# Gated stage: GpSimd's low parts interleaved and ternary weights in three steps; last stage: rows rounded at once, input rows turned ahead

## The chip, the cores and the metric

The kernel runs on one core of one Trainium2 chip. The metric is the device time of one execution, in microseconds (us). TensorE is called PE here, VectorE DVE, ScalarE ACT, GpSimd POOL and SyncE SP. All operands are fp32; where a product needs more than one pass, each operand is split into a high part and a low part that the kernel makes by itself.

## The reference

The program is a two-layer transformer block on `x` of 64 x 32 x 256. Each layer has a conditioned projection, attention, an adapter or expert product, and a feed-forward part. The diff touches two of them.

The gated stage (`mlp0`) is the second half of layer 0. A gated product with low-rank adapters chosen by `ada` (silu(x Wg + ...) times (x Wu + ...), times Wd) is followed by a gated feed-forward part with ternary weights:

```
def ternary_quant(w):
    s = jnp.mean(jnp.abs(w))
    q = jnp.clip(jnp.round(w / s), -1.0, 1.0) * s
    return w + jax.lax.stop_gradient(q - w)
```

The last stage (`mlp1`) is the second half of layer 1. Each batch element has one of 16 experts (`x @ W[id] + b[id]`), and then a feed-forward part in which rows and weights are rounded to 127 levels:

```
scale = jnp.max(jnp.abs(v), axis=axis, keepdims=True) / 127
q = jnp.clip(jnp.round(v / jnp.maximum(scale, 1e-8)), -127, 127)
```

The gate and up products take rounded `y`; the gated rows `h` are rounded again before the down product; the result is added to `x`.

## The kernel before, in words

Each engine has its program written out by hand, in order, and the engines are tied by counting semaphores. An engine runs its instructions strictly in the order written; a `wait_ge` holds all that stands behind it.

**Gated stage, `mlp0`.** The 2048 rows go in 4 steps of 512 (`NS`), `step(i)` of each engine; steps 1 and 2 are a hardware loop. A step has `FC` = 8 gated pieces of 128 hidden columns with their down product, then the adapter's mask, then `HC` = 6 pieces of the ternary feed-forward part (five of 128 hidden columns and one of 42). For each piece PE makes the gate and up products, ACT the tanh, DVE two gating products (L1320, L1326), ACT the high part (`h_high`, L1209), POOL the low part (`h_low`, L907; DVE makes the last ones itself), and PE the down product (`down`, `fdown`, L1097) from both. For the next step's adapters DVE masks `ugm` and `uum` (`choose`, L1315), ACT makes their high parts (`u_high`, L1196 and L1197) and POOL their low parts (`u_low`, L947 and L948). In `step` of POOL, `u_low(i + 1)` stands between the 7 low parts of the gated pieces and the 4 of the ternary ones. `gates(i + 1, 0)` on PE (L1066) is the first to need them; it stands near the end of the ternary part.

In step 0 DVE also prepares the ternary weights (`prepare`, L1386): sums of magnitudes, scales, and `ternary` (L1360) once each for w1, w3 and w2, w2 in two calls (1280 columns, and 42 rows of 256). They stand between the gating of pieces 5, 6 and 7, and those of w2 behind piece 7 and its low part. Behind them stand the adapter mask (L1412) and its low part (L1414), for which PE waits (L1130) before it can go on.

**Last stage, `mlp1`.** 16 rounds of 128 rows, `g`. In a round PE has `gate_up(g)` (12 matmuls on two high and low weight parts), `turn_h(g - 1)` (6 transposes of the rounded gated rows), `turn_y(g + 1)` (2), `experts(g + 2)` (17 matmuls), `turn_x(g + 3)` (2) and `down(g - 1)` (6). ACT copies out what was turned (`hT_out`, `yT_out`, `xT_out`) behind the two tanhs of `gate(g)`. DVE has `quantise(g - 1)` (row maximum L2187, three small ones, rounding L2196), `hidden(g)` (L2176, L2182), `front(g + 2)` (L2164 to L2172: maximum, scale and rounding of the expert product) and `back(g - 1)` (L2202, the output's scale). POOL adds the result to `x` (L1984) and SP stores it. `turn_x` and `turn_y` write the two halves of one PSUM bank, `XY`, so each waits until ACT has copied the other's last result out (L1999 to L2001, L2022 to L2025). The expert weights come by SP from a ring of eight rounds.

Of the kernel before, what the change touches and what calls it, by code (L numbers as in the profile page):

```python
# [812 lines left out]
def mlp0(nc, k, ctx, at, xres, raw, banks, hs, w, ada_i, following, ag, au, ad, bg, bu, bd, wd, w1, w3, w2):  # L813
# [125 lines left out]
    def gpsimd(pool):  # L939
        def b_low(n):  # L940
            pool.wait_ge(b_first, n + 1)
            cols = slice(n * F, (n + 1) * F)
            pool.tensor_tensor(w[1][:, 1, cols], b_raw[:, cols], w[0][:, 1, cols].bitcast(F32), ALU.subtract).then_inc(b_second, 1)

        def u_low(i):
            pool.wait_ge(u_first, i + 1)
            pool.tensor_tensor(u_p[0][1], ugm, u_p[0][0].bitcast(F32), ALU.subtract)  # L947
            pool.tensor_tensor(u_p[1][1], uum, u_p[1][0].bitcast(F32), ALU.subtract).then_inc(u_second, 1)  # L948

        def early(i):  # L950
            n = i - STEPS
            if n == -6:
                b_low(0)
            if n == -5:
                b_low(1)
                u_low(0)
            if n in (-4, -3):
                h_low(pool, n + 5, n + 4, slice(0, P), h_first, h_second)
            if n == -2:
                pool.wait_ge(at.a_mm, STEPS)  # L960
                pool.memset(ones[:, :], 1.0).then_inc(ones_set, 1)
                pool.memset(sums, 0.0).then_inc(ones_set, 1)

        def step(i, nxt=True, start=0):
            for m in range(start, FC - 1):
                h_low(pool, i * FC + m + 1, m, slice(0, P), h_first, h_second)
            if nxt:
                u_low(i + 1)
            for m in range(HC - 2):
                h_low(pool, i * HC + m + 1, m, slice(0, hw[m]), f_first, f_second)  # L970

        def main():
            step(0, start=2)
            with pool.Fori(1, NS - 1) as i:
                step(i)
            step(NS - 1, nxt=False)
        return early, main

    def tensor(pe):
# [48 lines left out]
        def early(i, part):  # L1028
            n = i - STEPS
            if n == -6:  # L1030
                turn_first(part)
            elif n == -5:
                rank_first(part)
            elif n == -4:
                gate_part(0, part, 0)
                if part == 1:
                    pe.wait_ge(b_second, 2)
                    pe.wait_ge(u_second, 1)
                    bias_part(0, 0, 0)
                    bias_part(0, 1, 0)  # L1040
            elif n in (-3, -2):
                gate_part(n + 4, part, 0)
                bias_part(n + 4, part, 0)
# [21 lines left out]

        def gates(i, m):  # L1066
            if m == 0:
                pe.wait_ge(u_second, i + 1)
            if m >= 2:
                pe.wait_ge(h_mul, i * FC + m - 1)  # L1070
            else:
                pe.wait_ge(f_h, i * HC + m - 1)
            for n in range(2):
                gate_part(m, n, m % 2)
                bias_part(m, n, m % 2)
# [89 lines left out]
    def scalar(act):  # L1165
# [26 lines left out]
            act.activation(w[0][:, 1, 2 * F:2 * F + FC * D], wd_raw, ACT.Copy).then_inc(wd_first, 1)  # L1192

        def u_high(i):
            act.wait_ge(u_mask, i + 1)
            act.activation(u_p[0][0], ugm, ACT.Copy)  # L1196
            act.activation(u_p[1][0], uum, ACT.Copy).then_inc(u_first, 1)  # L1197

        def gate_tanh(i, m, e):
            act.wait_ge(gate_mm, i * FC + m + 1)  # L1200
# [65 lines left out]
    def vector(dve):  # L1266
# [92 lines left out]

        def ternary(to, x, col, p=P):  # L1360

            link(dve.tensor_scalar(x, x, scl[0:p, col:col + 1], None, ALU.mult))
            dve.tensor_scalar(to, x, 0.5, None, ALU.is_gt)
            link(dve.tensor_scalar(x, x, -0.5, None, ALU.is_lt))
            return dve.tensor_tensor(to, to.bitcast(F32), x, ALU.subtract)

        def sizes():
            dve.wait_ge(tern_in, 64)
# [540 lines left out]
def mlp1(nc, k, xres, out, last):  # L1909
# [6 lines left out]
    with ExitStack() as ctx:  # L1916
# [79 lines left out]
        def _(pe):  # L1996
            def turn_x(g):
                if g >= 1:
                    pe.wait_ge(xT_ev, g)  # L1999
                if g >= 3:  # L2000
                    pe.wait_ge(yT_ev, g - 1)  # L2001
                for c in range(KD):
                    m = pe.transpose(XY[:, c * P:(c + 1) * P], xres[:, g, c * P:(c + 1) * P], k.ident[:, :])
                m.then_inc(xT_tr, 1)
# [15 lines left out]

            def turn_y(g):
                pe.wait_ge(y_rnd, g + 1)  # L2022
                pe.wait_ge(xT_ev, min(max(3, g + 2), G))
                if g >= 1:
                    pe.wait_ge(yT_ev, g)  # L2025
                for c in range(KD):
# [54 lines left out]
            pe.wait_ge(w2_first, 1)  # L2081
            for g in range(G):
                gate_up(g)
                if g >= 1:
                    turn_h(g - 1)
                else:
                    pe.wait_ge(w2_second, 1)
                    pe.wait_ge(dg_ev, 1)
                if g + 1 < G:
                    turn_y(g + 1)  # L2090
                if g + 2 < G:
                    experts(g + 2)
                if g + 3 < G:
                    turn_x(g + 3)
                if g >= 1:
                    down(g - 1)
            turn_h(G - 1)
# [3 lines left out]
        def _(act):  # L2101
# [38 lines left out]
            yT_out(0)  # L2140
            for g in range(G):
                gate(g)
                if g >= 1:
                    hT_out(g - 1)
                if g + 1 < G:
                    yT_out(g + 1)
                if g + 3 < G:
                    xT_out(g + 3)
            hT_out(G - 1)

        @block.vector
        def _(dve):
# [61 lines left out]
            dve.tensor_copy(sw2[:, :], DN[:, 0:D]).then_inc(dg_ev, 1)  # L2214
            front(1)
            for g in range(G):
                if g >= 1:
                    quantise(g - 1)
                hidden(g)
                if g + 2 < G:  # L2220
                    front(g + 2)
                if g >= 1:
                    back(g - 1)
            quantise(G - 1)
            back(G - 1)


# [142 lines left out]
```

## Time and profile before

| what | us |
|---|---|
| median of 3 runs | 1381.22 (1380.98 to 1381.8) |
| profiled execution, its own time | 1376.09 |
| its span | 1374.2 |
| PE busy | 1301.3 (95%) |
| DVE busy | 927.0 (67%) |
| POOL busy | 585.4 (43%) |
| ACT busy | 524.8 (38%) |
| mean granted clock of PE | 0.983 of full |

The span runs from the first to the last instruction of the profiled execution; the 1.9 us beside it lie around it. The gated stage's own steps lie between some 740 and 1068 us of the span, the last stage from about 1255 us to the end. All rows below give times from the start of the span. A matmul's duration in the rows is longer than the distance to the next one, since matmuls overlap: 512 columns follow each other every 0.23 us at full clock.

### The profile page before, as it was taken

The page shows a single profiled execution, that of the slowest core. Times are in us where ns is not written, and L with a number is a line of the kernel's source. Part 1 is how long each engine was busy: PE and PEld are TensorE (multiplying, and loading weights), DVE is VectorE, ACT ScalarE, POOL GpSimd, SP SyncE. Part 2 cuts the span into 40 slices and gives each one's busy share as a digit, 9 for nine tenths or more (in the row PEclk, how much of TensorE's full clock was granted, in tenths as well). Part 3 has the DMA queues.
Part 4 walks back from the last instruction along what each step waited for, and adds up shares of the span by engine and source line. Part 5 has one row for each costly group of instructions (what it writes and reads, how often), then busy time and mean ns, then how long its engine had stood idle before and what let it go on. Part 6 is the DMA issues. An engine that isn't in the chain of part 4 may idle for free. (4 is left out here: it accounts for less than half of the span.)

```text
span 1374.2 us, 37198 instructions
## 1 busy us (share of the span) xinstructions
PE 1301.3 (95%) x14870; PEld 1067.3 (78%) x14870; DVE 927.0 (67%) x1822; ACT 524.8 (38%) x1218; POOL 585.4 (43%) x688
## 2 busy tenths in 40 slices
PE   4999999999999999999999989999998799997997
PEld 3788888888888888888888877878786588886665
DVE  3888788877778888887887585252524356665886
ACT  3344444444444444444445313231313223332442
POOL 1755555555565555655556222122221223323111
PEclk9999999999999999999999999999999899997999
DMA  6000000010000100000010201000000540001610
GB/s 200 10 13 14 13 13 14 13 28 13 14 13 14 31 14 13 13 13 21 13 42 33 94 20 44 1 1 0 0 0 1 174 138 0 0 0 49 190 49 24
DMA packets 35532, 46.41 MB, mean 34 GB/s; under 512 B 7214, under 2 KB 24840, under 8 KB 35272
## 3 DMA queue, kind: packets, MB, share of 16 engines
q1 hardware_dynamic: 33048, 43.81, 10.6%
q8 instruction: 89, 1.46, 0.4%
q10 hardware_dynamic: 2272, 0.52, 0.2%
q14 instruction: 43, 0.35, 0.1%
q0 software_dynamic: 80, 0.26, 0.1%
HBM read 42.22 MB, written 2.36 MB: 32 GB/s over the span
## 5 line engine op out<-in xcount | busy, mean ns | idle before, releaser
L448 PE MATMUL OE<-w_o,ogT_s 128*128 128x256 f32 x512 | 137.7, 392 | 0.0
L907 POOL TENSOR_TENSOR hs_lo<-work,hs_hi 128x512 fp32r<-128x512 f32 x44 | 57.9, 1317 | 179.2 <-ACT hs_hi L1209 179.2
L250 POOL TENSOR_TENSOR turned<-raw 128x512 f32<-128x512 f32 x62 | 78.8, 1271 | 121.0 <-DVE raw L683 121.0
L708 DVE RECIPROCAL enz<-SC 128x128 f32<-128x128 f32 x128 | 121.2, 948 | 1.9 <-PE SC L396 1.8
L291 POOL TENSOR_TENSOR exz<-ex,enz 128x256 f32<-128x256 f32 x64 | 47.5, 742 | 133.2 <-ACT ex L611 133.2
L339 PE MATMUL PJ<-hs_hi,w_hi 128*128 128x512 f32 x248 | 101.5, 409 | 0.0
L350 PE MATMUL PJ<-w_hi,hs_hi 128*128 128x512 f32 x256 | 100.6, 393 | 0.0
L350 PE MATMUL PJ<-w_lo,hs_hi 128*128 128x512 f32 x256 | 100.2, 392 | 0.0
L350 PE MATMUL PJ<-w_hi,hs_lo 128*128 128x512 f32 x256 | 99.8, 390 | 0.0
L339 PE MATMUL PJ<-hs_hi,w_lo 128*128 128x512 f32 x248 | 97.2, 392 | 0.0
L339 PE MATMUL PJ<-hs_lo,w_hi 128*128 128x512 f32 x248 | 97.1, 392 | 0.0
L448 PEld LDWEIGHTS OE<-w_o,ogT_s 128*128 128x128 f32 x512 | 87.1, 189 | 11.1 <-issue 0.2
L541 ACT ACTIVATE pT_s<-AW_TA 128x256 f32<-128x256 f32 x64 | 24.6, 384 | 177.1 <-PE AW_TA L400 177.1
L611 ACT ACTIVATE ex<-ok,mn 128x64 f32<-128x64 f32 x256 | 68.2, 337 | 51.7 <-DVE mn L747 51.7
L683 DVE TENSOR_TENSOR raw<-PJ,cosb 128x512 f32<-128x512 f32 x124 | 82.1, 662 | 8.2 <-DMA idx_i<-in_ada 1.2
L683 DVE TENSOR_TENSOR raw<-PJ,sinb 128x512 f32<-128x512 f32 x124 | 84.3, 679 | 0.0
L251 POOL TENSOR_TENSOR turned<-raw 128x512 f32<-128x512 f32 x62 | 78.8, 1272 | 0.0
L1209 ACT ACTIVATE hs_hi<-work 128x512 fp32r<-128x512 f32 (+1 forms) x56 | 35.4, 631 | 97.9 <-DVE work L1326 82.4
L258 POOL TENSOR_TENSOR og<-og,rstd 128x512 f32<-128x512 f32 x64 | 67.0, 1047 | 5.0
L255 POOL TENSOR_TENSOR rstd<-mse,mhalf 128x4 f32<-128x4 f32 x64 | 65.2, 1019 | 7.0 <-DVE mse L737 7.0
L477 PE MATMUL OO<-raw,wm 64*64 64x128 f32 x1024 | 67.7, 269 | 0.1
L712 DVE SCALAR_TENSOR_TENSOR raw<-raw,PJ 128x512 f32<-128x512 f32 x64 | 44.0, 688 | 33.9 <-ACT raw L562 33.9
(413 smaller groups left out, 3475.0 us busy)
## 6 DMA issues: line engine op xcount, KB each, us to landing
we_ring<-in_we SPq DMA_DIRECT2D x64, 256.0 KB, 3.0
w_raw<-in_w_slices SPq DMA_DIRECT2D x64, 128.0 KB, 2.5
xres<-in_x SPq DMA_DIRECT2D x2, 1024.0 KB, 8.3
turned<-in_w_slices SPq DMA_DIRECT2D x4, 512.0 KB, 4.6
w_o<-in_wo SPq DMA_DIRECT2D x4, 512.0 KB, 5.1
out_rows<-xres SPq DMA_DIRECT2D x16, 128.0 KB, 1.7
w1r<-in_w1i SPq DMA_DIRECT2D x1, 1408.0 KB, 6.7
raw<-in_w SPq DMA_DIRECT2D x2, 682.0 KB
```

The costliest lines, as they stand in the source:

```text
L250: pool.tensor_tensor(to[:, 0, :], x1c[:, :], x2s[:, :], ALU.subtract)
L251: pool.tensor_tensor(to[:, 1, :], x2c[:, :], x1s[:, :], ALU.add).then_inc(qk_add, 1)
L255: pool.tensor_tensor(rstd[:, :], mse[:, :], mhalf[:, :], ALU.pow).then_inc(o_rstd, 1)
L258: pool.tensor_tensor(heads(og[:, :]), heads(og[:, :]), rstd[:, :].unsqueeze(2).to_broadcast([P, HQ, DK]), ALU.mult).then_inc(o_norm, 1)
L339: m = pe.matmul(banks_of(j)[half][:, :], w[:, slot, a:a + P], h[:, c, toks], start=(n == 0), stop=(n == len(terms) - 1))
L350: m = pe.matmul(bank[:, :], h[:, c, toks], w[:, slot, a:a + QW], start=(n == 0), stop=(n == len(terms) - 1))
L448: m = pe.matmul(OE[:, SW:SW + D], ogT_s[:, i % 2, h * P:(h + 1) * P], w_o[i // G % 2][:, h, :], start=(h == 0), stop=(h == HQ - 1))
L477: m = pe.matmul(OO[toks, h * P:(h + 1) * P], wm[toks, h, :], v_s[toks, i % 2, h * P:(h + 1) * P], start=True, stop=True, tile_position=(b ...
L611: act.activation(ex[:, cols], ok[:, cols], ACT.Exp, scale=-1.0, bias=mn[:, h:h + 1]).then_inc(ok_exp, 1)
L683: return dve.tensor_tensor(out_.rearrange(by, t=T), bank[:, :].rearrange(by, t=T), table[:, :].unsqueeze(1).to_broadcast([P, TOK // T, T]) ...
L708: dve.reciprocal(enz[:, cols], SC[:, SW:2 * SW][:, cols]).then_inc(z_rec, 1)
L907: eng.tensor_tensor(hT[1][s, m % 2, :], h[s, m % 2, :], hT[0][s, m % 2, :].bitcast(F32), ALU.subtract).then_inc(second, 1)
```

## The change

In the gated stage `u_high` and `u_low` are split in two halves, each with its own wait, and POOL takes the two halves behind the first and the second ternary piece. `ternary` multiplies and bounds above, bounds below and adds the rounding constant, and takes the constant off again: three instructions in place of four. In the last stage DVE rounds the gated rows of a round directly behind their gating. PE turns the input rows of round g + 3 directly behind the gate matmuls, and ACT copies them out directly behind the tanhs; the waits on the shared bank change with that.

```diff
@@ gpsimd, gated stage
-        def u_low(i):
-            pool.wait_ge(u_first, i + 1)
-            pool.tensor_tensor(u_p[0][1], ugm, u_p[0][0].bitcast(F32), ALU.subtract)
-            pool.tensor_tensor(u_p[1][1], uum, u_p[1][0].bitcast(F32), ALU.subtract).then_inc(u_second, 1)
+        def u_low(i, n):
+            pool.wait_ge(u_first, i * 2 + n + 1)
+            pool.tensor_tensor(u_p[n][1], (ugm, uum)[n], u_p[n][0].bitcast(F32), ALU.subtract).then_inc(u_second, 1)
...
-                u_low(0)
+                u_low(0, 0)
+                u_low(0, 1)
...
         def step(i, nxt=True, start=0):
             for m in range(start, FC - 1):
                 h_low(pool, i * FC + m + 1, m, slice(0, P), h_first, h_second)
-            if nxt:
-                u_low(i + 1)
             for m in range(HC - 2):
                 h_low(pool, i * HC + m + 1, m, slice(0, hw[m]), f_first, f_second)
+                if nxt and m < 2:
+                    u_low(i + 1, m)
@@ tensor, gated stage
-                    pe.wait_ge(u_second, 1)
+                    pe.wait_ge(u_second, 2)
...
-                pe.wait_ge(u_second, i + 1)
+                pe.wait_ge(u_second, i * 2 + 2)
@@ scalar, gated stage
         def u_high(i):
-            act.wait_ge(u_mask, i + 1)
-            act.activation(u_p[0][0], ugm, ACT.Copy)
-            act.activation(u_p[1][0], uum, ACT.Copy).then_inc(u_first, 1)
+            for n, ready in enumerate((ug_mask, u_mask)):
+                act.wait_ge(ready, i + 1)
+                act.activation(u_p[n][0], (ugm, uum)[n], ACT.Copy).then_inc(u_first, 1)
@@ vector, gated stage
         def ternary(to, x, col, p=P):
-            link(dve.tensor_scalar(x, x, scl[0:p, col:col + 1], None, ALU.mult))
-            dve.tensor_scalar(to, x, 0.5, None, ALU.is_gt)
-            link(dve.tensor_scalar(x, x, -0.5, None, ALU.is_lt))
-            return dve.tensor_tensor(to, to.bitcast(F32), x, ALU.subtract)
+            link(dve.tensor_scalar(x, x, scl[0:p, col:col + 1], 1.0, ALU.mult, ALU.min))
+            link(dve.tensor_scalar(x, x, -1.0, RND, ALU.max, ALU.add))
+            return dve.tensor_scalar(to, x, -RND, None, ALU.add)
@@ tensor, last stage
             def turn_x(g):
...
                 if g >= 3:
-                    pe.wait_ge(yT_ev, g - 1)
+                    pe.wait_ge(yT_ev, g - 2)
...
             def turn_y(g):
                 pe.wait_ge(y_rnd, g + 1)
-                pe.wait_ge(xT_ev, min(max(3, g + 2), G))
+                pe.wait_ge(xT_ev, min(g + 3, G))
...
             for g in range(G):
                 gate_up(g)
+                if g + 3 < G:
+                    turn_x(g + 3)
                 if g >= 1:
                     turn_h(g - 1)
...
                 if g + 2 < G:
                     experts(g + 2)
-                if g + 3 < G:
-                    turn_x(g + 3)
                 if g >= 1:
                     down(g - 1)
@@ scalar, last stage
                 gate(g)
+                if g + 3 < G:
+                    xT_out(g + 3)
                 if g >= 1:
                     hT_out(g - 1)
                 if g + 1 < G:
                     yT_out(g + 1)
-                if g + 3 < G:
-                    xT_out(g + 3)
@@ vector, last stage
             for g in range(G):
-                if g >= 1:
-                    quantise(g - 1)
                 hidden(g)
+                quantise(g)
                 if g + 2 < G:
                     front(g + 2)
                 if g >= 1:
                     back(g - 1)
-            quantise(G - 1)
             back(G - 1)
```

## Rows read from the trace of the kernel before

**Rows 1.** PE waits 735:1100: for whom, us in total, times, longest

```profile
PE AW_TA L1097 <- POOL hs_lo L907: 3.1, 3, 1.0
```

**Rows 2.** Timeline of PE and ACT, step 0: start us, us, what

```profile
812.07 0.39 PE L983 MATMUL OO<-hs_lo,w_hi 128*128 128x512 f32 x1
...
821.77 0.50 PE L983 MATMUL AW_TA<-hs_hi,bd_hi 128*128 128x512 f32 x1 [3.45 <-DVE hs_lo L1414]
...
813.22 0.63 ACT L1209 ACTIVATE hs_hi<-work 128x512 fp32r<-128x512 f32 x1 [2.06 <-DVE work L1326]
```

**Rows 3.** PE waits 1264:1374, columns as in rows 1

```profile
PE HT L2045 <- DVE hr L2196: 8.6, 15, 2.7
```

**Rows 4.** Timeline of ACT, POOL and PE, step 1, first ternary piece

```profile
904.03 0.63 ACT L1209 ACTIVATE hs_hi<-work 128x512 fp32r<-128x512 f32 x1 [0.44 <-DVE work L1326]
...
906.17 2.54 POOL L907 TENSOR_TENSOR hs_lo<-work,hs_hi 128x512 fp32r<-128x512 f32 x2
...
906.08 0.40 PE L1148 MATMUL PJ<-zT_lo,tern 128*128 128x512 f32 x1
...
907.50 0.39 PE L1097 MATMUL AW_TA<-tern,hs_hi 128*128 128x256 f32 x1 [1.02 <-POOL hs_lo L907]
```

**Rows 5.** Timeline of DVE, step 0, third matrix and mask

```profile
814.49 0.88 DVE L1362 TENSOR_SCALAR raw<-raw,work 128x1280 f32<-128x1280 f32 x1
...
816.15 0.82 DVE L1364 TENSOR_SCALAR raw<-raw 128x1280 f32<-128x1280 f32 x1
...
817.00 1.49 DVE L1365 TENSOR_TENSOR tern<-tern,raw 128x1280 fp32r<-128x1280 f32 x1
...
819.65 0.68 DVE L1412 TENSOR_TENSOR work<-TB,work 128x512 f32<-128x512 f32 x1
```

**Rows 6.** Busy time by stretch: PE, PEld, DVE, ACT, POOL, then granted clock, DMA

```profile
822.00:828.00 6.00, 6.00 (x20) 4.76 (x20) 3.08 (x6) 1.09 (x2) 0.00 (x0) 0.72 0.85 290
...
895.00:968.00 73.00, 71.79 (x339) 58.65 (x339) 28.50 (x45) 21.05 (x35) 16.61 (x13) 1.00 0.00 0
```

**Rows 7.** Timeline of PE, last stage, one round

```profile
1315.57 0.48 PE L2036 MATMUL GU<-w_hi,yqT 128*128 128x512 f32 x1
...
1318.03 0.33 PE L2037 MATMUL GU<-w_lo,yqT 128*128 128x384 f32 x1
...
1318.75 0.88 PE L2045 MATMUL HT<-ident,hr 128*128 128x128 f32 x6 [0.39 <-DVE hr L2196]
...
1319.46 0.38 PE L2027 MATMUL XY<-ident,y 128*128 128x128 f32 x2
...
1321.09 0.44 PE L2003 MATMUL XY<-ident,xres 128*128 128x128 f32 x2
...
1321.93 0.48 PE L2036 MATMUL GU<-w_hi,yqT 128*128 128x512 f32 x1
```

**Rows 8.** Timeline of ACT and DVE, the same round, and the end

```profile
1317.70 0.42 ACT L2117 ACTIVATE th<-GU,row 128x192 f32<-128x192 f32 x1 [0.23 <-PE GU L2037]
...
1321.56 0.38 ACT L2106 ACTIVATE xT<-XY 128x256 f32<-128x256 f32 x1 [0.81 <-PE XY L2003]
...
1316.50 0.88 DVE L2187 TENSOR_REDUCE row<-hr 128x1 f32<-128x704 f32 x1
...
1318.61 0.88 DVE L2176 SCALAR_TENSOR_TENSOR hh<-th,GU 128x704 f32<-128x704 f32 x1
...
1321.22 0.42 DVE L2164 TENSOR_REDUCE row<-Y 128x1 f32<-128x256 f32 x1 [0.81 <-PE Y L2017]
...
1364.86 0.48 DVE L2202 SCALAR_TENSOR_TENSOR xo<-DN,row,sw 128x256 f32<-128x256 f32 x1 [0.99 <-PE DN L2053]
```

**Rows 9.** Timeline of POOL and DVE, step 0, matrix two

```profile
807.58 1.95 POOL L907 TENSOR_TENSOR hs_lo<-work,hs_hi 128x512 fp32r<-128x512 f32 x1 [4.62 <-ACT hs_hi L1209]
...
830.55 1.29 POOL L947 TENSOR_TENSOR hs_lo<-work,hs_hi 128x512 fp32r<-128x512 f32 x1 [17.54 <-ACT hs_hi L1197]
...
808.28 1.97 DVE L1364 TENSOR_SCALAR raw<-raw 128x1364 f32<-128x1364 f32 x1
```

## Prediction

> **What bounds the kernel now.** I first read the table of busy time: TensorE (PE) is busy for 95% of the span, so a microsecond counts only where PE waits. Then I read whom PE waits for in the two stages that the diff touches. In the gated stage it waits three times 1.0 us for GpSimd's (POOL's) `hs_lo` of L907 [rows 1] and once 3.45 us for VectorE's (DVE's) `hs_lo` of L1414 [rows 2]. In the last stage it waits 15 times for DVE's rounded rows (L2196), 8.6 us in all, 2.7 of it the last time [rows 3]. The timelines show why.
>
> **The low parts.** In steps 0 to 2 POOL makes `u_low` as two subtractions of 1.3 us and only then the low part of the first gated piece. ACT has the high part of that piece ready at 904.66, but POOL starts its low part behind the two, at 906.17. PE's last matmul before it starts at 906.08 and the dependent one at 907.50, instead of one matmul spacing of 0.23 later, 906.31: 1.19 us lost [rows 4].
>
> **The ternary weights.** In the stage's first step DVE turns three weight matrices ternary, four instructions each, between its other duties. The third takes from 814.49 to 819.65, its 42-row rest included. Only then comes the mask L1412, and PE's matmul follows 2.12 us later, at 821.77 [rows 2, 5]. In the 6 us behind this wait the granted clock averages 0.72, so part of them runs at the lower of the two levels, 1.2 GHz [rows 6].
>
> **The last stage.** One round of 128 rows takes 6.36 us (1315.57 to 1321.93). PE issues its last gate matmul at 1318.03, could go on at 1318.20 (a 384-column slot, three quarters of 0.23) and goes on at 1318.75: 0.55 lost. DVE rounds the rows of round g-1 (from 1316.50) before it gates round g (from 1318.61), and then idles 0.81 us for PE's expert product. So the loop is rounding, PE's turn of the rows, experts, `front`, `back`, rounding [rows 7, 8].
>
> **The change, part by part.**
>
> *Interleaved low parts.* The first piece's low part no longer stands behind `u_low`. POOL is idle, so it runs from about 904.7 to 906.0 and PE needs it at 906.3: the wait goes, 1.17 us each, three times, **3.5 us**. What is late next? One `u_low` now stands before the second piece's low part. It ends near 907.3, and that low part ends now at 908.71 (906.17 + 2.54), so it ends no later than today. PE, 1.17 us earlier than now, asks for it after 8 matmuls of 0.23 and 8 of half that, near 909.1. The second `u_low` ends near 910 and is asked for only at the end of the step. ACT's split of `u_high` adds a wait and a signal per step, on semaphores long raised: nothing. The same edit at the end of the first layer is costed at nothing too, since PE has no wait for POOL there.
>
> *Three ternary steps.* All three are one-source operations in SBUF, like the three cheap ones now. On 1280 columns the rows have 0.88 for the scaling and 0.82 for an in-place comparison, where the two-source subtraction that goes takes 1.49. The third matrix becomes 0.88 + 0.82 + 0.82, the rest, a fifth as long, about 0.9 with its fixed costs: 3.45 instead of 5.16 us, **1.7**. The start moves as well. ACT's high part of the last gated piece waited for DVE until 813.22, because the first two matrices held DVE. They shrink by over 1.3 us each (one step of two sources goes, and the other comparison was slowed), so what releases it is PE's product ending behind 812.07, near 812.5: **0.7** [rows 2, 5]. PE resumes 2.4 us earlier. Bounds: with 1.49 for each step nothing (DVE would be no faster), and at most the whole 3.45.
>
> The price depends on POOL. The comparison that took 0.82 took 1.97 where a POOL subtraction ran beside it, and that subtraction took 1.95 instead of 1.29 [rows 9]. The sum: matrices one and two meet POOL and may take 3.9 us each, which is hidden, since DVE then still idles before the last gated piece. Matrix three meets none: POOL's next work is at 830.55 after 17.54 us of idling [rows 9]. The Trainium skill (SBUF — State Buffer, "The single rule") says that only one port pair is contended between VectorE and GpSimd, and that it is an exclusive lock. By that rule all three new steps can be blocked, where the old fourth, a two-source one, was no two-port operation; the edit would then gain nothing wherever POOL is busy, and the sum would be 2.4 smaller if it were so for matrix three.
>
> *Clock.* Of the 3.45 us of waiting 1.1 stay, or up to 1.6 if PE itself comes earlier. After the waits of 1.0 in the next steps the clock stayed at 1.00 [rows 6]. What stays is nearer to 1.0 than to 3.45, so I take full speed: 6 x 0.28 = 1.7 us come back, I count **1.6**. Bounds 0 and 1.7.
>
> *Last stage: rounding at once.* DVE now goes hidden(g), quantise(g), front(g+2), back(g-1). Its work in a round is 6.36 - 0.81 = 5.55 us, plus some 0.05 because the maximum now directly follows the product it reads. PE's work is 6.36 - 0.55 = 5.81. The rounded rows of g-1 are ready a round early, so PE leads [rows 7, 8]. DVE can start gating when ACT's second tanh is done, 2.55 us after the first gate matmul (1318.12), so at the earliest 5.81 + 2.6 = 8.4 after the round before began, and is free at 2.6 + 5.6 = 8.2. The slack is only 0.2 a round, but PE does not feel a late DVE before it is over 1 us late: it needs the rounded rows and `front` one round later.
>
> *Last stage: input rows ahead.* `turn_x` moves on PE to directly behind the gate matmuls, past `turn_h`, `turn_y` and `experts`, and `xT_out` on ACT past `hT_out` and `yT_out`. The work is the same. But `turn_y` now waits for this round's `xT_out`: PE to ACT takes 0.47 (1321.09 to 1321.56), the copy 0.38, back 0.1, together 0.95. The cover is `turn_h`, 0.71 (1318.75 to 1319.46), and a third of that for `turn_x`, 0.95 as well [rows 7, 8]. I charge 0.06 a round, bounds 0 and 0.2. Behind the waiting `turn_y` stand `experts` and `down`, all of it on PE's path. `yT_out` comes 0.8 us later than now, and the next gates need it later still. Round 0 has no `turn_h` as cover: 0.7 lost. No DMA is moved on SP's queue; its triggers only come earlier.
>
> Sum for the stage: 14 rounds x (0.55 - 0.06) = 6.9. The waits are 8.6 - 2.7 - 14 x 0.39 = 0.4 longer than the usual round's [rows 3], and go too. Round 0: -0.7. At the end `back(14)` no longer stands between the gating and the rounding of round 15: 0.99 idle and 0.4 work, +1.4 [rows 8]. Together **8.0 us**.
>
> **Total:** 3.5 + 2.4 + 1.6 + 8.0 = 15.5 us. The span goes from 1374.2 to 1358.7, the profiled execution from 1376.1 to 1360.6. The median of the runs shown lies 5.1 us above the profiled one, so I forecast 1381.2 - 15.5 = **1365.7**. About 0.2% (2.8 us) is what a measurement of this kernel can tell from no change.
>
> **The rivals.**
>
> *The clock stays low after the shortened wait.* For it: 1.6 is not 1.0, and an earlier short wait stands close before. 1365.7 + 1.6 = 1367.3. Chance 0.17.
>
> *The last stage keeps its pace.* DVE's slack of 0.2 a round is thin; POOL's addition, 0.7 us long, now falls beside the gating. If DVE lost 0.5 a round, it would end near 6.3: 14 x 0.45 = 6.3 less gain, 1372.0. Against: the two new neighbours share no buffer, and the gating reads one operand from PSUM. Chance 0.11.
>
> *The ternary steps are no cheaper,* so the change does not do there what it says: at 1.49 each, 2.4 + 1.6 are lost, 1369.7. Against: both cheap rows are single-source ones, as the new steps are. Chance 0.07.
>
> *Slower: the hand-over before `turn_y`.* It is the one wait that the change adds to PE in every round. It decides where the trip by ACT takes 2.3 us instead of 0.95: 14 x 1.35 = 18.9 us eat the 15.5 and leave 3.4, so 1384.6. ACT would have to reach `xT_out` late; but its second tanh ends at 1318.12, before PE is even through with the gates, so little speaks for it. Chance 0.03. The gains and this loss balancing, no visible change: 0.03.
>
> **How the numbers follow.** The forecast has 0.59; its own spread, from the hand-over, the spacings and the median against the profile, is about 2.5 us. With the clock rival and most of the partial cases the range is 1362.0 to 1371.5, about 2 in 10 outside. Faster by over 0.2% is all but the last two: 0.94.
>
> **What would show it.** Right: no PE wait for POOL's L907 in the ternary products; three instructions of under 0.95 us on the third matrix; a wait for L1414 of 1.0 to 1.7 us with the clock at 1.00 behind it; a round of 5.8 to 5.95 us; one PE wait for L2196 in all; DVE idle for tanh, not for the expert product. Wrong: a round over 6.1 us, POOL beside the third matrix, or a low clock behind the L1414 wait.

## Result, and the profile of the changed kernel

| | before | changed |
|---|---|---|
| median, us | 1381.1 (1377.18 to 1381.8, 4 runs) | 1362.34 (1359.39 to 1365.58, 4 runs) |
| profiled execution, us | 1376.09 | 1359.39 |
| its span, us | 1374.2 | 1357.5 |
| mean granted clock of PE | 0.983 | 0.985 |

The ratio is 0.987, with a 95% interval of 0.9846 to 0.9894: 18.8 us or 1.3% faster. Forecast were 15.5 us and 1365.7, with 1362.0 to 1371.5 as the range, so the result lies 0.3 us inside its lower end. Below, lines of the changed kernel stand one lower than before from L1366 on, because one line of `ternary` went: L1413 is the old L1414, L2195 the old L2196.

The page of the changed kernel begins with the engines' busy times:

```profile
PE 1296.2 (95%) x14870; PEld 1067.4 (79%) x14870; DVE 921.7 (68%) x1818; ACT 524.8 (39%) x1218; POOL 586.0 (43%) x688
```

PE's busy time, 1301.3 before, fell by 5, the span by 16.7: most of what went was waiting. The waits of PE in 735 to 1100 us (columns as in rows 1):

```profile
PE AW_TA L983 <- DVE hs_lo L1413: 2.3, 2, 1.5
```

The line of [rows 1], three waits for POOL, is gone, and the 3.45 us of [rows 2] is a wait of 1.5. The waits of PE in 1240 to 1360 us, the last stage:

```profile
PE HT L2044 <- DVE hr L2195: 1.5, 1, 1.5
...
PE XY L2026 <- ACT xT L2105: 0.7, 1, 0.7
```

Of the 15 waits for the rounded rows [rows 3] one is left, behind the last round, and `turn_y` has one wait that it did not have, in round 0.

To see where the time went I cut each execution at six events. They are, in the timelines of DVE and PE of the changed kernel:

```profile
799.02 0.15 DVE L1376 COPY work<-OE 128x4 f32<-128x4 f32 x1
...
824.05 0.42 PE L1148 MATMUL PJ<-zT_hi,tern 128*128 128x512 f32 x1
...
1039.48 0.50 PE L1148 MATMUL PJ<-zT_hi,tern 128*128 128x512 f32 x1 [2.50 <-DVE zT_lo L1418]
...
1060.18 0.48 DVE L1436 SCALAR_TENSOR_TENSOR xres<-OE,work,xres 128x256 f32<-128x256 f32 x1
...
1259.73 0.47 PE L2035 MATMUL GU<-w_hi,yqT 128*128 128x512 f32 x1 [0.56 <-ACT yqT L2109]
...
1354.12 0.48 DVE L2201 SCALAR_TENSOR_TENSOR xo<-DN,row,sw 128x256 f32<-128x256 f32 x1 [2.31 <-PE DN L2052]
```

The first starts the ternary scales, the second ends step 0's ternary wait, the third lies in the last gated step, the fourth ends the gated stage, the fifth is the first gate product and the sixth the last `xo`. The differences of these start times, us, one profiled execution each:

| kernel | start to scales | step 0 | to the last step | end of gated stage | next attention | last stage |
|---|---|---|---|---|---|---|
| before | 798.60 | 29.02 | 219.29 | 21.39 | 198.06 | 104.44 |
| changed | 799.02 | 25.03 | 215.43 | 20.70 | 199.55 | 94.39 |
| changed, again (e10) | 801.86 | 24.99 | 215.45 | 21.07 | 202.68 | 95.73 |
| e1 low parts alone | 798.97 | 28.98 | 215.43 | 21.09 | 202.60 | 104.45 |
| e2 ternary alone | 798.23 | 24.99 | 219.38 | 21.17 | 199.22 | 104.44 |
| e3 rounding at once alone | 799.07 | 28.99 | 219.33 | 21.08 | 199.00 | 94.50 |
| e4 turning ahead alone | 801.37 | 28.99 | 219.32 | 21.46 | 200.78 | 105.99 |
| e5 copy late | 799.57 | 24.98 | 215.42 | 20.89 | 199.85 | 110.53 |
| e6 third matrix ahead | 800.94 | 23.51 | 215.40 | 21.75 | 199.54 | 95.15 |
| e7 one step more | 800.44 | 25.98 | 215.44 | 21.39 | 200.72 | 94.29 |
| e8 two steps more | 799.39 | 28.43 | 215.41 | 20.77 | 199.84 | 95.27 |
| e9 three parts, third matrix ahead | 802.41 | 23.52 | 215.46 | 20.65 | 203.52 | 94.19 |

Step 0 and the stretch behind it repeat within 0.1 us between kernels that are alike there. The two stretches that no edit touches, the first and the attention, vary by 4.2 and 5.5 us. So the stretches say what an edit does; a total of one execution can't, to a few us.

The changed kernel against before: step 0 -3.99, the steps behind it -3.86, the stage's end -0.69, the last stage -10.05; the untouched stretches +0.42 and +1.49. That is -16.7, the difference of the profiled executions.

**Step 0.** Timeline of PE and ACT of the changed kernel [rows 2]:

```profile
819.80 0.50 PE L983 MATMUL AW_TA<-hs_hi,bd_hi 128*128 128x512 f32 x1 [1.54 <-DVE hs_lo L1413]
...
812.98 0.63 ACT L1209 ACTIVATE hs_hi<-work 128x512 fp32r<-128x512 f32 x1 [1.41 <-PE OO L983]
```

And of DVE, the third matrix [rows 5]:

```profile
814.25 0.88 DVE L1362 TENSOR_SCALAR raw<-raw,work 128x1280 f32<-128x1280 f32 x1
815.17 0.83 DVE L1363 TENSOR_SCALAR raw<-raw 128x1280 f32<-128x1280 f32 x1
816.03 0.83 DVE L1364 TENSOR_SCALAR tern<-raw 128x1280 fp32r<-128x1280 f32 x1
...
817.68 0.68 DVE L1411 TENSOR_TENSOR work<-TB,work 128x512 f32<-128x512 f32 x1
```

The three steps take 0.88, 0.83 and 0.83 us, and from the first to the mask it is 3.43 instead of 5.16. ACT's high part now waits for PE, not for DVE. The busy time of all engines in the 6 us behind the wait, columns as in [rows 6]:

```profile
822.00:828.00 6.00, 6.00 (x27) 4.80 (x26) 3.86 (x6) 2.96 (x7) 0.00 (x0) 1.00 0.80 259
```

The clock stays at 1.00, and 27 instead of 20 matmuls fall into the 6 us.

**Low parts.** Timeline of POOL and PE in step 1, first ternary piece [rows 4]:

```profile
899.91 1.30 POOL L907 TENSOR_TENSOR hs_lo<-work,hs_hi 128x512 fp32r<-128x512 f32 x1 [16.93 <-ACT hs_hi L1209]
...
901.17 1.29 POOL L947 TENSOR_TENSOR hs_lo<-work,hs_hi 128x512 fp32r<-128x512 f32 x1
901.24 0.39 PE L1148 MATMUL PJ<-zT_lo,tern 128*128 128x512 f32 x1
...
901.47 0.28 PE L1097 MATMUL AW_TA<-tern,hs_hi 128*128 128x256 f32 x1
```

POOL makes the piece's low part (L907) first and half of `u_low` (L947) behind it, and PE goes on after 0.23 us instead of 1.42.

**Last stage.** One round of PE, ACT and DVE [rows 7, 8]:

```profile
1296.42 0.34 PE L2036 MATMUL GU<-w_lo,yqT 128*128 128x384 f32 x1
1296.55 0.74 POOL L1983 TENSOR_TENSOR xres<-xres,xo 128x256 f32<-128x256 f32 x1 [0.92 <-DVE xo L2201]
1296.55 0.89 DVE L2175 SCALAR_TENSOR_TENSOR hh<-th,GU 128x704 f32<-128x704 f32 x1
1296.60 0.38 PE L2002 MATMUL XY<-ident,xres 128*128 128x128 f32 x2
...
1296.82 0.82 PE L2044 MATMUL HT<-ident,hr 128*128 128x128 f32 x6
1297.02 0.39 ACT L2105 ACTIVATE xT<-XY 128x256 f32<-128x256 f32 x1 [0.49 <-PE XY L2002]
...
1297.50 0.41 PE L2026 MATMUL XY<-ident,y 128*128 128x128 f32 x2
...
1301.87 0.42 ACT L2116 ACTIVATE th<-GU,row 128x192 f32<-128x192 f32 x1 [0.23 <-PE GU L2036]
...
1302.32 0.89 DVE L2175 SCALAR_TENSOR_TENSOR hh<-th,GU 128x704 f32<-128x704 f32 x1
1302.37 0.38 PE L2002 MATMUL XY<-ident,xres 128*128 128x128 f32 x2
```

From `turn_x` to `turn_x` it is 5.77 us, and PE is without a wait. DVE too has almost no idle time left: it starts gating at 1302.32, 0.08 us after `back` ends and 0.03 after tanh does. The gating beside POOL's 0.74 us addition takes 0.89, against 0.88 in [rows 8], where it stood alone.

### The profile page after: what moved, and what is told of

It is laid out like the page before. It is cut to its first block and busy times, and to the rows that moved or that the text cites. A ratio compares the mean times of both kernels' runs of the same rounds, so it can differ in the third digit from the quotient of the medians.

```text
span 1357.5 us, 37198 instructions
## 1 busy us (share of the span) xinstructions
PE 1296.2 (95%) x14870; PEld 1067.4 (79%) x14870; DVE 921.7 (68%) x1818; ACT 524.8 (39%) x1218; POOL 586.0 (43%) x688
## 3 DMA queue, kind: packets, MB, share of 16 engines
q8 instruction: 89, 1.46, 0.5%
## 5 line engine op out<-in xcount | busy, mean ns | idle before, releaser
L907 POOL TENSOR_TENSOR hs_lo<-work,hs_hi 128x512 fp32r<-128x512 f32 x44 | 57.0, 1296 | 220.7 <-ACT hs_hi L1209 219.9
```

The lines of the kernel that those rows point to most:

```text
L907: eng.tensor_tensor(hT[1][s, m % 2, :], h[s, m % 2, :], hT[0][s, m % 2, :].bitcast(F32), ALU.subtract).then_inc(second, 1)
```

## Experiments

In all of them the kernel before ran beside on the same chip: e1 to e4 on one, e5 to e8 on a second, e9 and e10 on a third.

### e1: the low parts alone

```diff
 # gpsimd, on the kernel before
-            if nxt:
-                u_low(i + 1)
             for m in range(HC - 2):
                 h_low(pool, i * HC + m + 1, m, slice(0, hw[m]), f_first, f_second)
+                if nxt and m < 2:
+                    u_low(i + 1, m)
```

> Only the low parts are interleaved. My theory: PE's three waits of 1.0 us for POOL's hs_lo go and nothing takes their place, 3.5 us off the 1381 (ratio 0.9975), PE's first fdown product follows the matmul before it by 0.23 us. Rival (the second piece's low part or the next gates become late): a new PE wait in steps 0 to 2 of 0.5 us or more each, gain under 2 us.

1377.06 us (10 runs) against 1380.48 (25), ratio 0.997, interval 0.9957 to 0.9982. The stretch behind step 0 shrinks from 219.33 (middle of before, e2, e3 and e4) to 215.43: 3.9 us for three waits. That is 0.3 more than three times 1.19. PE's first matmul behind a wait is also followed late: after 0.22 us in the kernel before (907.50 and 907.72), and after 0.12 in the changed kernel, where there is no wait (901.47 and 901.59). This 0.1 goes three times too. Step 0 (28.98) and the last stage (104.45) don't move.

### e2: the ternary steps alone

```diff
 # vector, on the kernel before
+            link(dve.tensor_scalar(x, x, scl[0:p, col:col + 1], 1.0, ALU.mult, ALU.min))
+            link(dve.tensor_scalar(x, x, -1.0, RND, ALU.max, ALU.add))
+            return dve.tensor_scalar(to, x, -RND, None, ALU.add)
```

> Only the ternary weights are made in three steps. My theory: PE's wait for L1414 goes from 3.45 to about 1.5 us, PE resumes 2.4 us earlier and the 6 us behind it run at the full clock, another 1.6 us: 4.0 us off (ratio 0.9971). Rival (the clock follows the wait anyway, or is not tied to it): 2.4 us, with 0.43 us matmul spacings behind the wait.

1377.71 us (10 runs), ratio 0.9973, interval 0.9961 to 0.9986. PE's wait for L1413 is 1.50 us, with the matmuls behind it 0.23 apart, so the rival with the low clock is out here. Step 0 takes 24.99 instead of 29.02, so 4.0 us, and the next stretch stays at 219.38: the three waits for POOL are still there. The first two edits are independent and add up, to the 7.85 us that step 0 and the stretch behind it lose in the changed kernel.

### e3: rounding at once alone

```diff
 # vector, on the kernel before
             for g in range(G):
-                if g >= 1:
-                    quantise(g - 1)
                 hidden(g)
+                quantise(g)
 ...
-            quantise(G - 1)
```

> Only DVE's order in the last stage: the gated rows are rounded directly behind their gating, the input rows are turned in the old place. If this edit carries the stage's whole gain, the round is 5.75 to 5.85 us, PE waits for L2196 once (1.5 us), no wait for ACT's xT in round 0, and the stage is 8 to 9 us shorter (ratio 0.994). If the turning ahead is needed too, PE waits for ACT's yqT before turn_x, 0.2 us or more a round, and the round stays over 6.0 us, under 6 us gained.

1368.74 us (4 runs), ratio 0.9918, interval 0.9891 to 0.9946. The last stage takes 94.50 us, the changed kernel 94.39. In the timeline of PE, with `turn_x` still behind the experts, the first gate matmul, then one round's last gate matmul, `turn_h` and `turn_y`, and the last `turn_h`:

```profile
1267.47 0.47 PE L2036 MATMUL GU<-w_hi,yqT 128*128 128x512 f32 x1 [0.56 <-ACT yqT L2110]
...
1303.70 0.34 PE L2037 MATMUL GU<-w_lo,yqT 128*128 128x384 f32 x1
...
1303.88 0.82 PE L2045 MATMUL HT<-ident,hr 128*128 128x128 f32 x6
...
1304.53 0.38 PE L2027 MATMUL XY<-ident,y 128*128 128x128 f32 x2
...
1358.69 0.88 PE L2045 MATMUL HT<-ident,hr 128*128 128x128 f32 x6 [1.51 <-DVE hr L2196]
```

`turn_h` follows the last gate matmul after 0.18 us and nothing waits; the round is 5.76 us. DVE's order alone carries the whole gain of the stage, 9.9 us where I had expected 8 to 9. It even carries a little more than the change does: from the first gate matmul to the last `turn_h` it is 91.22 us here (1267.47 to 1358.69) and 91.74 in the changed kernel (1259.73 to 1351.47). That the whole stages come out alike is the clock: the last `down` ran at the lower clock here (1.46 us) and not in the changed kernel's first profile (0.83).

### e4: turning ahead alone

```diff
 # tensor, on the kernel before (scalar: xT_out moves likewise)
                 gate_up(g)
+                if g + 3 < G:
+                    turn_x(g + 3)
                 if g >= 1:
                     turn_h(g - 1)
```

> Only the input rows are turned ahead, DVE rounds in the old order. If the rounding loop through DVE binds, turn_x (0.24 us) only fills PE's wait of 0.55: the round stays at 6.36, round 0 loses 0.7, ratio 1.000 to 1.001. If turn_x or the hand-over was part of the loop, the round falls by 0.2 us or more, 3 us gained.

1381.55 us (10 runs), ratio 1.0007, interval 0.9994 to 1.002: no change that the totals could tell. The timeline of PE shows why nothing is gained:

```profile
1299.16 0.38 PE L2003 MATMUL XY<-ident,xres 128*128 128x128 f32 x2
1299.97 0.88 PE L2045 MATMUL HT<-ident,hr 128*128 128x128 f32 x6 [0.43 <-DVE hr L2196]
...
1305.52 0.38 PE L2003 MATMUL XY<-ident,xres 128*128 128x128 f32 x2
```

`turn_x` fills a part of PE's wait for the rounded rows, but those come when DVE has them, and the round stays at 6.36 (1299.16 to 1305.52). The last stage is 1.55 us longer. In round 0 `turn_y` starts 1.07 us later after the first gate matmul (3.69 instead of 2.62): 0.67 is its wait for `xT_out`, the rest `turn_x` itself and the gap around it. The experts' product, DVE's `front` and the first `turn_h` are all late by that (8.97 instead of 7.87), more than the 0.7 that I had expected. The other 0.4 is a `turn_h` of the last round at the lower clock (1.31 instead of 0.88).

### e5: the copy behind the rounded rows

The rival on the slower side lives from a trip of the input rows over ACT of 2.3 us. This kernel makes it about that long.

```diff
 # scalar, on the changed kernel
                 gate(g)
-                if g + 3 < G:
-                    xT_out(g + 3)
                 if g >= 1:
                     hT_out(g - 1)
+                if g + 3 < G:
+                    xT_out(g + 3)
```

> The changed kernel, but ACT copies the turned input rows out behind hT_out instead of ahead of it. My slower rival says the hand-over before turn_y decides from a trip of 2.3 us on. Theory: ACT reaches xT_out only after hT_out (PE's turn_h 0.9, the copy 0.8), so turn_y waits 1.3 to 1.5 us for ACT's xT in each round 1 to 12, the round is 7.1 to 7.3 us, and the time is 15 to 18 us longer than the changed kernel's, near 1379. Rival (PE has slack that hides it): a round under 6.2 us.

1376.55 us in one run. PE and ACT in one round:

```profile
1297.19 0.38 PE L2002 MATMUL XY<-ident,xres 128*128 128x128 f32 x2
...
1298.97 0.38 ACT L2105 ACTIVATE xT<-XY 128x256 f32<-128x256 f32 x1
...
1299.45 0.41 PE L2026 MATMUL XY<-ident,y 128*128 128x128 f32 x2 [1.22 <-issue]
```

and the waits of PE in the stage, where the hand-over comes first ("issue": the profile names no releaser; what the wait follows is ACT's copy, 1298.97 and 0.38 us long):

```profile
PE XY L2026 <- issue: 14.7, 12, 1.2
```

The trip from `turn_x` to `turn_y` takes 2.26 us, and the round 7.13 (1292.66 to 1299.79, its bias matmuls). The wait is 1.22, a little under the 1.3 that I had expected. The prediction's formula gives 5.87 + 1.35 = 7.22 for 2.3. The price of the rival was right for a round, and its condition is only one ACT instruction in the wrong place away. Its 14 rounds were too many: `turn_x` runs in rounds 0 to 12 only, and the table has 12 waits. The last stage is 16.1 us longer than the changed kernel's; the one run is 1376.55 against a median of 1362.34, 14.2.

### e6: the third matrix ahead of the last low part

```diff
 # vector, on the changed kernel
-                    if m < FC - 1:
-                        prepare(m)
+                    prepare(m)
 ...
-            if isinstance(i, int) and i == 0:
-                prepare(FC - 1)
```

> The changed kernel, but the third weight matrix is made ternary ahead of the last gated piece's low part, in DVE's idle 3.5 us there. Theory: the matrix and its rest (3.45 us) fit the gap, the mask follows PE's adapter product, and PE's wait for L1413 in step 0 goes from 1.5 us to under 0.3: 1.3 to 1.5 us less than the changed kernel in that stretch, ratio to the kernel before 0.9855 to 0.9862. Rival (the low part of the last piece gets late): PE waits up to 1.5 us for DVE's hs_lo L907 in its place, no gain.

1363.12 us (4 runs), ratio 0.9882, interval 0.9862 to 0.9902. PE's wait in step 0 is gone:

```profile
819.71 0.60 PE L1000 MATMUL AW_TA<-ident,x_st 128*128 128x128 f32 x4
820.24 0.50 PE L983 MATMUL AW_TA<-hs_hi,bd_hi 128*128 128x512 f32 x1
```

Step 0 takes 23.51 us, 1.5 less than the changed kernel's, though one of the third matrix's steps now meets POOL and takes 1.83. In the total the 1.5 us can't be seen, and the ratio misses the 0.9855 to 0.9862 that I had expected: in this execution the clock was low at the end of the gated stage (21.75 instead of 20.70) and of the last one (95.15 instead of 94.39).

### e7 and e8: the wait made longer

One instruction of 0.83 us behind the third matrix's last step, and two of them, lengthen the wait in small steps.

```diff
 # vector, on the changed kernel; range(1) in e7, range(2) in e8
-                ternary(t2[:, 0:full, :], w2_s[:, 0:full, :], 5)
+                link(ternary(t2[:, 0:full, :], w2_s[:, 0:full, :], 5))
+                for _ in range(1):
+                    link(dve.tensor_scalar(t2[:, 0:full, :], w2_s[:, 0:full, :], -RND, None, ALU.add))
```

> The changed kernel with the last ternary instruction of the third matrix done once more (0.87 us), to see how long a wait costs PE its clock. The wait for L1413 becomes 2.4 us. Theory (the clock falls somewhere between a wait of 1.5 and one of 3.45): cannot tell yet; if it falls, the stretch from the wait's end to the first ternary matmul takes 5.8 instead of 4.25 us. If the clock does not depend on this wait, 4.25.

> The same with two more instructions of 0.87 us: a wait of 3.3 us, as long as the 3.45 of the kernel before. Theory: the clock falls as before, 5.7 to 5.9 us from the wait's end to the first ternary matmul. Rival (the clock behind the wait was tied to something else, such as the phase of the run): 4.25 us.

1363.54 and 1364.42 us in one run each. Timeline of PE in e7, the wait and the first product behind it:

```profile
822.20 0.50 PE L983 MATMUL AW_TA<-hs_hi,bd_hi 128*128 128x512 f32 x1 [2.49 <-DVE hs_lo L1415]
...
826.42 0.43 PE L1148 MATMUL PJ<-zT_hi,tern 128*128 128x512 f32 x1
```

and in e8:

```profile
822.01 0.50 PE L983 MATMUL AW_TA<-hs_hi,bd_hi 128*128 128x512 f32 x1 [3.39 <-DVE hs_lo L1415]
...
827.82 0.39 PE L1148 MATMUL PJ<-zT_hi,tern 128*128 128x512 f32 x1
```

Behind 2.49 us of waiting the same 18 matmuls take 4.22 us, as behind 1.54 in the changed kernel (4.25). Behind 3.39 us they take 5.81, as in the kernel before (5.85, from 821.77 to 827.62): for a while they follow each other every 0.43 instead of 0.23 us. So step 0 grows by 0.95 us in e7 and by 3.40 in e8, 1.8 of it the two instructions and 1.6 the clock. This is one profile of each; the last section has a wait of 2.50 us that is followed by either clock, so e7 doesn't show that 2.49 us is always free.

### e9: three of the four parts, with the third matrix ahead

The changed kernel with `turn_x` and `xT_out` where they stood before, and e6's edit. e10 is the changed kernel, unaltered, beside it.

> The changed kernel without its fourth part (input rows turned where they stood before) and with the third matrix's steps ahead of VectorE's last low part. Theory: the last stage owes everything to VectorE's order, so it keeps its 94.4 to 94.6 us from the first gate matmul to the last xo, with no 0.7 us wait of turn_y for the copy xT_out in round 0; the first step of the gated stage has no wait for the mask's low part, 1.5 us less than the changed kernel from the scale copy to the first product of zT with a ternary matrix (25.0 there). Total 1.0 to 1.6 below the changed kernel of this same call, if the clock is dealt alike. Rival (turning ahead was needed beside the new order): rounds of over 5.9 us and a last stage of 96 us or more, slower than the changed kernel by over 0.5. Where the same 2.5 us wait for zT_lo of the last gated step leaves the clock low, 1 us is lost by chance in either kernel.

1363.31 us (1359.37 to 1365.04, 4 runs), ratio 0.9861, interval 0.984 to 0.9883. Step 0 takes 23.52, as the theory has it. The last stage takes 94.19, a little under its 94.4, with no wait of `turn_y` for the copy in round 0. And here the last `down` ran at the lower clock (1.46 us): up to the last `turn_h` the stage takes 90.91 us, against 91.74 and 91.79 in the two profiles of the changed kernel. So by the stretches this version is ahead by 1.5 + 0.8 us, and turning ahead is not only unneeded beside the new order but costs 0.5 (e3) to 0.8 us. The medians side by side differ by 2.6 (1363.31 and 1365.88), with intervals that overlap; by the totals it is not proven.

### e10: the changed kernel again

> The changed kernel once more, unaltered, beside the run before it on the same chip. Theory (the clock behind waits of about 2.5 us is dealt differently from run to run): a median within 1361.5 to 1364.5, single runs spread over 4 us or more, and the time falls as the mean granted clock rises, by some 0.9 us for 0.001 of clock. Rival (the spread is noise with no cause in the clock): runs at equal clock differ by over 3 us. The last stage takes 94.4 us in any case, and what differs from the first profile lies behind waits.

1365.88 us (1363.22 to 1367.07, 4 runs), ratio 0.9883, interval 0.9864 to 0.9902. The median lies outside what I expected, and the spread of 3.9 us within three runs at a clock of 0.980 speaks for the rival as far as these four go: the clock alone doesn't set the time (that it is given to 0.001 only may hide about 1 us of it, by the slope in the last section). The table shows what else differs from the first profile: 2.8 us before the ternary scales and 3.1 in the attention, both untouched. In the attention PE's 4878 matmuls keep it busy for 181.2 us in e10 and for 179.7 in the first profile, at a mean clock of 0.90 and 0.91, and it stands idle 1.6 us longer: half of the difference at most is the clock.

The last stage, which I had put at 94.4 "in any case", took 95.73: `turn_h(15)` and the last `down` ran at the lower clock (1.54 and 1.46 us, 0.87 and 0.83 in the first profile). Step 0 and the stretch behind it came out as in the first profile within 0.04 us.

## Why the prediction was right, and what was off

**The direction and the bound.** PE bounded the kernel, and what shortened its waits shortened the kernel, nearly one for one.

**Low parts: 3.5 forecast, 3.9 measured** (219.33 to 215.43, the same in all eight kernels with the edit). The waits were counted right, three of 1.19 (the sum took 1.17 of each); what was missing is the slower restart of PE behind each wait, 0.1 us. The second `u_low`, which I had ending near 910 and asked for late, held nobody up.

**Ternary steps and clock: 2.4 + 1.6 forecast, 4.0 measured** (29.02 to 25.03). The instructions cost what the nearest one-source rows said. The rival that they are no cheaper is out. The remaining wait was put at 1.1 to 1.6 and is 1.54. The clock rival is out for this wait: at 1.50 to 1.54 us the clock stayed full behind it in all four profiles (changed, e2, e5, e10). e8 shows that it falls behind 3.39, at the same place in the kernel, so it is the length that decides there. e7 had the clock full behind 2.49, in one profile.

**What POOL does to these steps.** The sum had matrices one and two meet POOL. Only matrix one did. Timeline of the changed kernel, DVE and POOL in the first matrix:

```profile
801.36 0.87 DVE L1363 TENSOR_SCALAR raw<-raw 128x1364 f32<-128x1364 f32 x1
801.88 1.50 POOL L907 TENSOR_TENSOR hs_lo<-work,hs_hi 128x512 fp32r<-128x512 f32 x1 [5.08 <-ACT hs_hi L1209]
802.27 1.84 DVE L1364 TENSOR_SCALAR tern<-raw 128x1364 fp32r<-128x1364 f32 x1
```

POOL's subtraction takes 1.50 instead of 1.30, and DVE's step, issued 1.1 us before POOL ends, takes 1.84 instead of 0.87: it ends 0.73 us behind POOL. With the exclusive lock that the Trainium skill describes (SBUF — State Buffer, "The single rule") the trace agrees to 0.15 us: first POOL gives way until DVE's step ends at 802.23, then DVE until POOL ends at 803.38. In matrix two the steps take 0.92, 0.87 and 0.87, since POOL starts only at 808.00, when the third (from 807.21) is all but done. Both were hidden, as the sum had it. As forecast, matrix three met none of it and the price of the rule was not paid. One of nine steps is hit.

The prediction also took the old fourth step, the two-source one, out of what can meet POOL. The kernel before shows otherwise, in matrix two:

```profile
810.28 1.58 DVE L1365 TENSOR_TENSOR tern<-tern,raw 128x1364 fp32r<-128x1364 f32 x1
...
811.23 1.77 POOL L907 TENSOR_TENSOR hs_lo<-work,hs_hi 128x512 fp32r<-128x512 f32 x1 [1.71 <-ACT hs_hi L1209]
```

Beside it POOL's subtraction takes 1.77 instead of 1.29 us, so the new steps did not bring in a contention that the old ones were free of.

**The end of the gated stage** has 0.69 us that no step of the prediction named. It is not the edits': the stretch is 21.09 and 21.17 in e1 and e2, 21.08 in e3, and between 20.65 and 21.75 over all. It is luck of the clock. From the end of the 2.50 us wait to the first matmul behind the last wait it is 18.98 us in the kernel before (1046.91 to 1065.89), with the lower clock behind the wait, and 18.25 in the changed one (1039.48 to 1057.73), with the full clock. e1 and e2 have the full clock there and the lower one behind the last wait (see the last section).

**Last stage: 8.0 forecast, 10.05 measured.** The mechanism of the rounding was right, the size of the stage was off in three terms.

- The step "I charge 0.06 a round" for the hand-over, and PE's work in a round of 5.81: the round was to be 5.87 and is 5.77, below the 5.8 to 5.95 that I had named. `turn_y` finds the copy ready: from `turn_x` to the copy's start it is 0.42 us, not 0.47, and with the 0.39 of the copy the trip is about 0.9, the cover 0.90 (1296.60 to 1297.50). Without a wait for the rounded rows the slower restart behind it goes too, as in the low parts: from `turn_h` to `turn_y` it is 0.71 in [rows 7] and 0.65 in e3. So PE's work in a round is 5.76 (e3) and not 5.81, and the hand-over adds 0.01 and not 0.06. 0.10 a round over the 11 rounds that run steadily is 1.1 us.
- The last rounds: once PE sets the pace, rounds with less PE work are shorter. From `turn_h` to `turn_h` the changed kernel has 5.56, 5.5, 4.92 and 4.05 us at the end, the kernel before 6.36, 6.36, 5.3 and 5.3: 3.3 us less, where the forecast's rounds and end together give some 2.9. That is 0.4.
- The clock at the end: the last `down` takes 0.83 instead of 1.46, 0.6 us. The forecast owes nothing to it and the change perhaps neither. With the old order this `down` was slow in all four profiles, with the new order in five of eight (e3, e6, e8, e9, e10); whether the shorter wait ahead of it (1.50 instead of 2.69) helps is not shown. In e10, with a slow end, the stage took 95.73, 8.7 less than before.

**Turning ahead** costs more here than it brings, and the prediction didn't say so. Its sum has the two prices (0.06 a round, 0.7 in round 0) and no gain beside them, but it never says that the change would be better without this part. Measured are 0.01 a round and 0.7 of waiting in round 0. Taken alone the move makes the stage 1.1 us longer up to the first `turn_h` (e4). Taken away it makes it shorter by 0.5 to 0.8 (e3, e9), to the last `turn_h`, which in the changed kernel is

```profile
1351.47 0.87 PE L2044 MATMUL HT<-ident,hr 128*128 128x128 f32 x6 [1.50 <-DVE hr L2195]
```

**DVE's slack** was thin, as the rival had it, and is used up: DVE idles 0.08 us ahead of the gating. But PE's work is as long, and the stage didn't keep its pace.

**The slower rival** is the one that a small slip would have made true: e5 has a hand-over of 2.26 us, a round of 7.13, and loses 16.1 us of the stage.

**The median.** I took the offset of the median from the profiled execution as fixed, at 5.1 us; beside the changed kernel it was 3.0. That is 2.1 of the 3.4 us by which the first result lies under the forecast, and chance. All eight runs of the changed kernel have their median at 1364.5, the eleven of the kernel before beside them 1381.2: 16.7 us, between the forecast and the first result. Most of the distance from 15.5 to 18.8 is such variation; the stretches put the edits' own worth at 3.9 + 4.0 + 8.7 to 10.1 for the last stage, so 16.6 to 18.0. That the forecast is near has some luck in it too: the last stage gave more than its 8.0, and the untouched stretches took 1.9 us back.

## What to carry to other kernels

Where an engine is busy 95% of the span, follow each of its waits to the instruction queue that holds the awaited result back: two of the three gains here came from the order in which another engine did the same work, and the third from fewer passes over the same data. Moving work of the bounding engine into its own wait gains nothing while the awaited result comes no earlier, so move the producer first; then look whether the second move still brings anything, since here it costs 0.5 us or more. Where single executions differ by more than an edit is worth, cut them at fixed events and compare the stretches: 0.1 us could be told here, and in the totals 2 us could not.

## What the runs showed of the hardware

**The same wait is followed by either clock.** In the last gated step PE waits 2.50 us for `zT_lo` in all twelve profiles above. In six the matmuls behind it keep their spacing of 0.23 us (the changed kernel, e1, e2, e5, e8, e9), in six a part follows every 0.43 (before, e3, e4, e6, e7, e10). Timeline of PE behind this wait in the changed kernel:

```profile
1040.29 0.40 PE L1148 MATMUL PJ<-zT_lo,tern 128*128 128x512 f32 x1
...
1041.22 0.39 PE L1148 MATMUL PJ<-zT_lo,tern 128*128 128x512 f32 x1
```

and in the kernel before:

```profile
1046.91 0.50 PE L1148 MATMUL PJ<-zT_hi,tern 128*128 128x512 f32 x1 [2.50 <-DVE zT_lo L1419]
...
1047.78 0.63 PE L1148 MATMUL PJ<-zT_lo,tern 128*128 128x512 f32 x1
...
1049.48 0.63 PE L1148 MATMUL PJ<-zT_lo,tern 128*128 128x512 f32 x1
```

The duration is 0.63 at the lower of the two levels and 0.39 at the upper. Four matmuls take 0.93 us (1040.29 to 1041.22) or 1.70 (1047.78 to 1049.48). The first twelve matmuls or so cost up to 1.6 us more. Part of that is taken back, since PE's later waits for VectorE's last low parts get shorter (1.38 us in the kernel before, 0.46 + 1.49 in the changed one): the stretch to the end of the stage is on average 20.88 us in the first six and 21.36 in the others. The Trainium skill says that the moment of a change of clock varies from run to run, because what the chip looks at does not start with the kernel (TensorE: Matmul & The Clock Gate, "What's actually happening"). The traces agree: one kernel, the changed one, has both outcomes (changed and e10). So the matmuls behind a wait of 2.5 us may take up to 1.6 us more or nothing. In step 0 a wait of 1.5 did not cost it in any of four profiles, and one of 3.4 did in all five kernels that have it (before, e1, e3, e4, e8), by the length of step 0.

A wait of 1.5 us is not always free, though. At two places where another wait stands close before it, the clock fell in some profiles: behind the last wait of the gated stage (1.47 and 1.48 us in e1 and e2, with one of 0.45 ahead) the matmuls soon follow each other every 0.21 instead of 0.12 us, and behind the last wait for rounded rows (1.5 us, with one of 0.90 ahead and one behind) the last `down` took 1.46 instead of 0.83 us in five of eight profiles.

**Executions of one kernel differ, partly with the granted clock.** Over the eight runs of the changed kernel the time falls by 1.1 us for each 0.001 of mean clock (1359.39 us at 0.985, 1367.00 at 0.979; correlation -0.92), over 25 of the kernel before by 0.7 (correlation -0.68). What remains at equal clock, up to 3.9 us, I did not explain.
